# A two-layer graph network on a dense 8192 x 8192 adjacency: no late diagonal product, one ScalarE stop a row, combinations behind the first strip

## The reference

```python
h = maximum(layernorm(x), 0)
T0 = h; T1 = L @ T0; T2 = 2 * (L @ T1) - T0; T3 = 2 * (L @ T2) - T1
x = x + T0 @ w0 + T1 @ w1 + T2 @ w2 + T3 @ w3        # Chebyshev layer, K = 4
h = maximum(layernorm(x), 0)
deg = clip(sum(L, axis=1) + 1, 1)
neigh = (L @ h + h) / deg
out = maximum(concat(h, neigh) @ W + b, 0)
x = x + out / maximum(norm(out, axis=1), 1e-12)      # SAGE layer
```

## Time and profile before

| | |
|---|---|
| median of 3 runs | 2723.29 us |
| lowest, highest | 2719.33, 2724.41 us |
| profiled execution, its own time | 2724.01 us |
| its span | 2722.2 us |
| TensorE matmul busy | 2173.2 us (80%) |
| VectorE busy | 1667.8 us (61%) |
| GpSimd (gather issue) busy | 1269.6 us (47%) |
| ScalarE busy | 688.7 us (25%) |
| moved by DMA | 690.08 MB, mean 253 GB/s |
| mean granted TensorE clock | 0.892 |

### The profile page before, as it was taken

How to read it: one execution, slowest core, us unless ns; L and a number is a source line. 1 busy time by engine, 2 the same in 40 slices (tenths; PEclk the granted TensorE clock), 3 DMA queues, 4 the chain that set the end, 5 groups by cost and what they waited for, 6 DMA issues and landing times.

```text
span 2722.2 us, 29753 instructions
## 1 busy us (share of the span) xinstructions
PE 2173.2 (80%) x12008; PEld 1683.9 (62%) x12008; DVE 1667.8 (61%) x1328; ACT 688.7 (25%) x1667; POOL 1269.6 (47%) x1357
## 2 busy tenths in 40 slices
PE   2567777787888899888886899687867999998785
PEld 1344445566666677767775788566655877775453
DVE  7565555573555555466534575557465687779886
ACT  3342222222221222255111132535121122120000
POOL 4554444434444434074422363534332576667771
PEclk9787777889888899889898899788988999999887
DMA  9797777756766667587744698867766899999995
GB/s 280 263 310 235 248 243 247 247 186 231 269 242 243 200 210 258 171 216 248 263 149 191 234 317 249 241 208 212 257 223 226 266 365 340 332 338 360 364 277 182
DMA packets 220747, 690.08 MB, mean 253 GB/s; under 512 B 47554, under 2 KB 78274, under 8 KB 220610
## 3 DMA queue, kind: packets, MB, share of 16 engines
q0 software_dynamic: 163840, 652.30, 70.2%
q1 hardware_dynamic: 51776, 34.64, 5.0%
q10 hardware_dynamic: 4994, 1.25, 0.3%
HBM read 685.97 MB, written 2.10 MB: 253 GB/s over the span
## 4 chain that ended last, share of the span: by engine, by line
PE 56%; DVE 20%; POOL 7%; issue 6%; DMA 6%; ACT 4%; SPq 1%; ACTq 0%; DVEq 0%; POOLq 0%
PE ps_pair L815 40%; DVE ring L666 17%; PE ps_single L821 10%; POOL ring L408 7%; DMA ring<-in_adj_dram,index 5%; ACT ring L457 3%; PE ps_lin L757 1%; PE ps_lin L760 1%; SPq L379 1%; PE ps_single L719 1%; DMA ring<-in_adj_dram 1%; PE ps_lin L759 0%; PE ps_tr L776 0%; PE ps_lin L773 0%; PE ps_late L730 0%
## 5 line engine op out<-in xcount | busy, mean ns | idle before, releaser
L408 POOL DMA_INDIRECT ring<-in_adj_dram,index x1344 | 1268.1, 944 | 1400.4 <-PE ps_pair L815 514.7
L666 DVE STREAM_TRANSPOSE ring<-ring 128x2048 f32<-128x2048 f32 (+8 forms) x702 | 1466.6, 2134 | 705.6 <-ACT ring L457 605.5
L815 PE MATMUL ps_pair<-ring,vec 128*128 128x256 f32 x5760 | 1356.8, 397 | 266.0 <-DVE ring L666 253.7
L815 PEld LDWEIGHTS ps_pair<-ring,vec 128*128 128x128 f32 x5760 | 1137.4, 200 | 473.2 <-issue 197.8
L821 PE MATMUL ps_single<-ring,vec 128*64 128x256 f32 x4672 | 605.7, 413 | 267.0 <-DVE ring L666 261.3
L457 ACT ACTIVATE ring<-ring 128x1024 f32<-128x1024 f32 (+7 forms) x736 | 576.4, 786 | 405.6 <-DMA ring<-in_adj_dram,index 401.0
L821 PEld LDWEIGHTS ps_single<-ring,vec 128*64 128x64 f32 x4672 | 347.3, 148 | 491.6 <-issue 223.7
L480 ACT ACTIVATE sum_s<-ps_single 128x512 f32<-128x512 f32 x64 | 37.9, 593 | 745.1 <-PE ps_single L821 544.0
L457 ACT ACTIVATION_READ_ACCUMULATOR ring<-ring 128x1 f32 x736 | 139.1, 189 | 0.0
L638 DVE TENSOR_TENSOR res<-res,ps_late 128x256 f32<-128x256 f32 x12 | 5.1, 422 | 178.4 <-PE ps_late L730 178.4
L468 ACT ACTIVATE vec_t<-ps_xt 64x512 f32<-64x512 f32 x32 | 18.7, 584 | 294.5 <-PE ps_xt L709 294.5
(11 more groups left out here) (91 smaller groups left out, 551.3 us busy)
## 6 DMA issues: line engine op xcount, KB each, us to landing
ring<-in_adj_dram,index POOLq DMA_INDIRECT x1344, 7.2
ring<-in_adj_dram SPq DMA_DIRECT2D x160, 96.0 KB
ring<-in_adj_dram SPq DMA_DIRECT2D x160, 64.0 KB
ring<-in_adj_dram SPq DMA_DIRECT2D x160, 32.0 KB, 8.0
out_dram<-vec SPq DMA_DIRECT2D x64, 32.0 KB, 7.9
res<-in_x_dram SPq DMA_DIRECT2D x4, 256.0 KB, 8.2
res<-in_x_dram ACTq DMA_DIRECT2D x4, 256.0 KB, 8.7
tmp<-in_L_gnn_weight_dram ACTq DMA_DIRECT2D x2, 64.0 KB
```

Source lines behind the costliest of these rows:

```text
L408: pool.indirect_dma_start(strip_of(i)[:, g, :], None, adj_q, bass.IndirectOffsetOnAxis(ap=index[:, 0:1], axis=0), element_offset=(QN * (g ...
L666: nc.vector.transpose(blocks, blocks).then_inc(s_turned, 1)
L815: last = nc.tensor.matmul(ps_pair[n % 2][:, cells], vec[:, CB * J + c, :, :], moving, start=(pair == 0), stop=(pair == pairs - 1))
```

## The change

Five things are done:

- **No late product.** `late_product`, both `late_epilogue`s, `copy_diagonal`, `sum_d` and their semaphores are gone (with `ps_late`, whose PSUM becomes `ps_deg`). In sweep 1 only the units of `latest` stand behind. Sweep 2 loads the diagonal block in all 16 rows, as a single with T1: 24 more half-blocks (12.6 MB), and its combination gets the product of `sum_s` (L763 in the old numbering) in 12 more rows, with an evacuation of `ps_single`.
- **ScalarE.** For row n it sums all strips of the row, and the first strip of row n + 1 if its place is free more than two units before the end of row n; then it copies `vec_t`, then it evacuates. In sweep 1 it then stops once a row.
- **TensorE** combines row n not one unit into row n + 1, but up to a whole strip (in sweep 1 after 4 units), as far as the estimated time to the unit that needs the row's result leaves `LATENCY`.
- **VectorE** combines row n after the turning of the strip that follows (`end_step`; in sweep 1 after 8 steps, two strips, of row n + 1) in place of a count of units.
- **Strips** are at most 10 blocks wide in place of 12. In sweeps 2 and 3 there are 88 strips, 76 of them wide, in place of 78 and 66: rows of 11 and 12 blocks are now cut in two.

The diff, cut to its core (the removed functions are named above):

```diff
-WIDE = 12
+WIDE = 10
...
-LATE_BLOCKS = NB - 4
-LATE = 7
-NEXT = 1
-LEAD = 5
+LATENCY = {1: 14.0, 2: 14.0, 3: 20.0, 4: 0.0}
+BLOCK_COST = (0.86, 1.72)
 STORE_LAG = 12
-SUM_LEAD = 4
...
-                (behind if latest in Js or self.has_late and C in Js else early).append((k, Js))
+                (behind if latest in Js else early).append((k, Js))
...
     for C in reversed(range(NB)):
-        first = C + 1 if C < LATE_BLOCKS else C
-        runs = split(first, NB - 1)
+        runs = split(C, NB - 1)
...
-        ahead = {needed_row(rows[n + 1], J) for J in rows[n + 1].units[0][1]}
-        epilogue_at.append(row_start[n + 1] + (n not in ahead))
...
-    begin_at = [min(epilogue_at[n] + LEAD, first_need.get(n, n_units) + 1,
-                    (epilogue_at + [n_units])[n + 1] + NEXT) for n in range(len(rows))]
+    strip_at = list(itertools.accumulate((i for _, i, _ in units), max))
+    cost_to = [0.0] + list(itertools.accumulate(sum(BLOCK_COST[rows[n].kind(J)] for J in Js) for n, _, Js in units))
...
+        need = first_need.get(n, n_units)
+        at = row_start[n + 1]
+        while at < min(units_to[first_strip[n + 1] + 1], row_start[n + 2] - 1) and \
+                cost_to[need] - cost_to[at + 1] >= LATENCY[rows[n].sweep]:
+            at += 1
+        epilogue_at.append(at)
+        ahead = strip_at[at - 1]
+        while ahead < strip_at[at] and free_at[ahead + 1] < at:
+            ahead += 1
+        end_step.append(steps_to[ahead + 1])
...
             for n, row in enumerate(rows):
-                sum_rows(row_start[n] + SUM_LEAD)
+                ahead = first_strip[n + 1]
+                if n + 1 < len(rows) and free_at[ahead] + 2 < row_start[n + 1]:
+                    ahead += 1
+                sum_rows(ahead)
                 if n in x_rows:
...
-                if n - 1 in late_at:
-                    sum_rows(late_at[n - 1] + SUM_LEAD)
-                    act.wait_ge(s_late, late_rows.index(n - 1) + 1)
...
-                    nc.scalar.activation(sum_d[:], ps_single[(n - 1) % 2][:], ACT.Copy).then_inc(s_lateev, 1)
-                sum_rows(row_start[n + 1] + 1)
                 act.wait_ge(s_unit, row_start[n + 1])
...
                 if n in root_rows:
-                    sum_rows(begin_at[n])
+                    sum_rows(steps_to.index(end_step[n]))
...
                     nc.vector.transpose(blocks, blocks).then_inc(s_turned, 1)
-                    u = units_to[i] + (units_to[i + 1] - units_to[i]) * (p + 1) // steps_of[i]
-                    if rows[n].has_late and i + 1 == first_strip[n + 1] and p + 1 == steps_of[i]:
-                        copy_diagonal(n)
-                    if ended < begun and u >= min(begin_at[ended] + 1, n_units):
+                    step = steps_to[i] + p + 1
+                    if ended < begun and step > end_step[ended]:
                         epilogue_end(ended)
                         ended += 1
-                    if begun < len(rows) and ended == begun and u >= begin_at[begun]:
+                    while begun < len(rows) and ended == begun and step >= end_step[begun]:
                         epilogue(begun)
...
-                    if late < len(late_rows) and ended > late_rows[late] and u >= min(late_end_at[late_rows[late]] + LEAD,
-                                                                                      row_start[late_rows[late] + 2]):
-                        late_epilogue(late_rows[late])
...
-                    if n - 1 in late_at and u == late_at[n - 1]:
-                        late_product(n - 1)
-                    if n - 1 in late_at and u == late_end_at[n - 1]:
-                        late_epilogue(n - 1)
...
-                    if row.has_late and row.C in Js:
-                        pe.wait_ge(s_copied, late_rows.index(n) + 1)
```

More of the change, by code:

```diff
@@ L82, in __init__ @@
         self.sweep, self.C, self.pieces, self.final = sweep, C, pieces, final
-        self.has_late = sweep == 1 and C < LATE_BLOCKS
         early, behind = [], []
@@ L207, in needed_row @@
         return row_index[3, J]
-    epilogue_at = []
-    for n in range(len(rows)):
-        if n + 1 == len(rows):
-            epilogue_at.append(n_units)
-            continue
-        ahead = {needed_row(rows[n + 1], J) for J in rows[n + 1].units[0][1]}
-        epilogue_at.append(row_start[n + 1] + (n not in ahead))
     first_need = {}
@@ L223, in cheb_sage_kernel @@
             first_need.setdefault(needed_row(rows[n], J), u)
[L224 to L225 removed]
+    strip_at = list(itertools.accumulate((i for _, i, _ in units), max))
+    cost_to = [0.0] + list(itertools.accumulate(sum(BLOCK_COST[rows[n].kind(J)] for J in Js) for n, _, Js in units))
+    epilogue_at, end_step = [], []
+    for n in range(len(rows)):
+        if n + 1 == len(rows):
+            epilogue_at.append(n_units)
+            end_step.append(steps_to[-1])
+            continue
+        need = first_need.get(n, n_units)
[8 more added lines that the diff above has]
+        end_step.append(steps_to[ahead + 1])
     def sums_of(n):
@@ L441, in _, with sum_rows @@
             summed = [0]
-            def sum_rows(u):
-                while summed[0] < len(sum_strips) and strip_first[sum_strips[summed[0]]] < u:
+            def sum_rows(strip):
+                while summed[0] < len(sum_strips) and sum_strips[summed[0]] < strip:
                     i = sum_strips[summed[0]]
@@ L711, in transpose_vector @@
                 xts[0] += 1
-            def late_product(n):
-                C = rows[n].C
-                need_rows(n + 1)
-                for c in range(CB):
-                    half = F * (c % 2)
-                    last = nc.tensor.matmul(ps_single[n % 2][half:half + F, :], vec[:, CB * C + c, 1, :],
-                                            diagonal(C, c), start=(c < 2), stop=(c >= CB - 2))
-                last.then_inc(s_late, 1)
-            def late_epilogue(n):
-                late = late_rows.index(n)
-                pe.wait_ge(s_lateev, late + 1)
-                if late:
-                    pe.wait_ge(s_lateadd, late)
-                for c in range(CB):
-                    D = sum_d[:, P * c:P * c + P]
-                    last = nc.tensor.matmul(ps_late[:, c, :, :], D, rhs_s2[:], start=True, stop=True)
-                last.then_inc(s_latelin, 1)
             def epilogue(n):
```

49 lines of the change are left out of this document (3 added, 46 removed).

## The result

| | before | after |
|---|---|---|
| median of 4 runs each, us | 2721.47 (2719.33 to 2724.41) | **2499.06** (2497.35 to 2504.45) |
| profiled execution / its span, us | 2724.0 / 2722.2 | 2497.35 / 2495.5 |
| mean granted clock | 0.892 | 0.931 |

The ratio is 0.9185 [0.9168, 0.9203]. The forecast was 2522 (2440 to 2625), so the sum is off by 23 us. The terms behind the sum were further off: sweep 1 gained 87 us more than forecast, and sweeps 2 and 3 lost 63 more.

What follows compares the result with a forecast made beforehand. Sweep 1 was taken to be bound by two program-order stops, not an engine. Sweep 1 -209, sweep 2 +4, sweep 3 -6, last +10 sum to -201 us: 2523 from the profiled 2724.0, 2522 as median; range 2440 to 2625.

Steps and rivals of the forecast that it cites:

- two stops in order of program: Sweep 1: waits at VectorE's late addition and ScalarE's copy of vec_t bind it, not an engine; removing them saves 209 us.
- ScalarE's stop: Sweep 1, row C = 6: ScalarE stands 21.87 us at vec_t's copy, second strip's sums behind; TensorE then waits 9.61.
- The first stop: Sweep 1, row C = 6: VectorE stands 12.96 us before the late addition, next row's turning behind; TensorE stands 6.99.
- First the prices: Unit costs for the sum: pair half-block 1.88 us, single 1.04, a unit 3.8 or 2.1, turning a half-block 1.1.
- T+17.2, T+35, T+49.7: Sweep 1, rows C = 1 to 7, us from row start: VectorE's combination done, two strips turned, TensorE's five further units done.
- more than forecast: Rival, chance 0.15: loads flow, rows 1 to 7 at 48.5 us, 8 to 12 at 56; 286 us less, 2438.
- 25 + 19 - 10 = +34: Sweep 2, diagonal: 24 singles +25 us, the sum_s product in 12 more rows +19, idle time filled by added products -10.
- -48 + 18 = -30: Sweep 2, narrower strips: stops of rows C = 5 and 4 go, -48 us; new waits at C = 6 and 7, +18.
- VectorE's combination ahead of the next strip's turning costs back about 8: Sweep 3: this cost of about 8 us against about 14 saved by cutting rows C = 10 and 11, giving -6.
- Half the gain: Rival, chance 0.18: VectorE's new wait and low clock keep sweep 1's rows 1 to 7 at 61 us; 2621 in all.
- The gathers: Rival, chance 0.06: GpSimd's queue binds sweeps 2 and 3; 80 more gathers cost 99 us, giving 2621.
- Slower: Rival, chance 0.03: ScalarE's sums ahead of the evacuation hold up TensorE's combination in 16 rows, 395 us more, 2917.

Runs made afterwards that it cites:

- old_places_w12: The kernel before without the late product, with ScalarE's new order; combinations in their old places, strips up to 12 blocks; quick chip: 2483.82 us, ratio 0.9133.
- late_off_act: The kernel before without the late product, with ScalarE's new order, old combination places, strips up to 12 blocks; slow chip: 2905.98 us, ratio 0.9593.
- old_places_w10: The kernel before without the late product, with ScalarE's new order, old combination places, strips up to 10 blocks; quick chip: 2408.10 us, ratio 0.8853.
- old_places_w8: The kernel before without the late product, with ScalarE's new order, old combination places, strips up to 8 blocks; quick chip: 2349.96 us, ratio 0.8646.
- second set: Quick-chip runs of the changed kernel again (2497.47 us) and, with old combination places, strips up to 12, 10 and 8 blocks (2483.82, 2408.10, 2349.96 us).
- tensor_place_new: Against late_off_act_w10, TensorE's combination alone moved to the changed kernel's place, VectorE's and ScalarE's left as before; slow chip: 3103.28 us, ratio 1.0274.
- late_off_act_w10: The kernel before without the late product, with ScalarE's new order, old combination places, strips up to 10 blocks; slow chip: 2860.33 us, ratio 0.9436.
- late_off: The kernel before with only the late product removed, its diagonal moved to sweep 2; slow chips: 3000.48 us, ratio 0.9877; repeated, 2977.94 us, 0.9865.

## Why the prediction was right, and where it was not

**Right as a total, by two errors that offset.** The forecast of 2522 is 23 us above 2499, inside the range, and the cause it named for the gain, two stops in order of program in sweep 1, is borne out as a pair: old_places_w12 takes only the late product and ScalarE's old order away, and its sweep 1 takes 805 us, not 1110. ScalarE's stop is also shown alone, by late_off_act. The first stop's own part stays open: with the late product go the late stop, the ring places of the held block (some 40 us) and 33 us of TensorE's work (19.4 + 13.3 in the earlier trace rows), and no run takes these apart.

**Sweep 1: -209 forecast, -296 measured.** The mechanism was right, and the prices were not. The term that was mis-sized goes back to "First the prices": I took pair, single and combination from means over the whole kernel or from a stretch at the low clock, and the change itself lifts the clock. In rows 8 to 12, before and after (groups by line in the windows 583.2 to 945.8 and 425.1 to 681.3):

```profile
L815 PE MATMUL ps_pair<-ring,vec 128*128 128x256 f32 x801 | 202.1, 413 | 70.7 <-DVE ring L666 70.7
```

```profile
L736 PE MATMUL ps_pair<-ring,vec 128*128 128x256 f32 x801 | 177.2, 380 | 3.4 <-DVE ring L621 3.4
L742 PE MATMUL ps_single<-ring,vec 128*64 128x256 f32 x484 | 55.5, 382 | 0.1
```

A pair half-block is 177.2/100 = 1.77 us there, not 1.88, a single one 55.5/60.5 = 0.92, not 1.04, and the combination 4.7, not 7.7. My own sum for C = 10 with these, 20 x 1.77 + 12 x 0.92 + 4.7 + 1.0, gives 52.1 us; 50.3 was measured, and I had 58.8. For rows 1 to 7 the chain T+17.2, T+35, T+49.7 holds step by step in row C = 5: VectorE begins to turn at T+14.1 (3.1 us earlier, the combination), has both strips at T+31.8, and the row ends 14.9 us later, at T+46.7 (323.8). The 1.7 us of low clock wasn't there. The average of 48.5 is then set by the loads, near the bound of 47.3. By group: row 0 16 forecast, 19 measured (58 to 39); rows 1 to 7 114 and 139; rows 8 to 12 68 and 106; rows 13 to 15 11 and 32, the last since TensorE's busy time fell too, 189.3 to 176.3, with the clock from 0.92 to 1.00. This is what the rival "more than forecast" said of sweep 1 (48.5 for rows 1 to 7), with too little for the others.

**Sweep 2: +4 forecast, +26 measured.** old_places_w12 and w10 split it. The diagonal, forecast as 25 + 19 - 10 = +34 us, came to +61 (556 to 617, with the old places and 12 blocks; ScalarE's order is in it too). The narrower strips, -48 + 18 = -30, came to -55. The places of the combinations, to which I gave no cost in this sweep, are +16. In the +61 TensorE's busy time grew by 40 us (475.5 to 515.2), near the 25 + 19 of the forecast; what failed is "Some of the remaining idle time is filled by the added products: -10", for its idle time grew by 21 instead (80.5 to 101.9). The two stops of C = 5 and 4 are gone as forecast (46.8 and 42.6 us for 62.7 and 65.9 of the earlier trace rows), and the stop moved to C = 7 and 6 as forecast, but larger than 18:

```profile
1052.12 14.71 PE L736 MATMUL ps_pair<-ring,vec 128*128 128x256 f32 x56 [8.38 <-DVE ring L621]
1070.05 0.94 POOL L392 DMA_INDIRECT ring<-in_adj_dram,index  x1 [30.66 <-PE ps_pair L736]
1092.25 3.33 PE L736 MATMUL ps_pair<-ring,vec 128*128 128x256 f32 x7 [19.54 <-DVE ring L621]
```

GpSimd's gather is held 30.66 us until a strip is free, and TensorE stands 8.38 and 19.54 us, 27.9 in all, and 9.4 more in C = 6. old_places_w8, where TensorE doesn't stand at all in these rows, shows that this was the choice of 10 and not a price of narrow strips.

**Sweep 3: -6 forecast, +35 measured.** This is the one term with the wrong sign. The strips gave -21 (I had -14), and the late product and ScalarE's order together +9 (728 to 737), for which I have no account. The step that failed is "VectorE's combination ahead of the next strip's turning costs back about 8": the places cost 47. I counted the place of VectorE's four operations but not that it would stand there for TensorE's, which the change had moved too, nor ScalarE's root with sums queued behind it. How the 47 split between the three engines' places isn't shown on the quick chip.

**Last sweep: +10 forecast, +9 measured.** VectorE waits 39.5 us in 16 waits for L700 (above), 2.5 each, which is the 16 x 2.5 of the forecast; it waited 13.8 in 5 before. Only part of it reached the path; the places alone cost 13 in the second set.

**The other rivals.** Half the gain didn't come: TensorE's waits in rows 1 to 7 of sweep 1 were 2.2 us on average (36.8 in 17), and the clock stayed up, 0.94 there. The gathers did not bind (second set); "no run here shows 320 KB" overlooked that the kernel before has strips of 5 blocks too, in row C = 10 of sweep 2 and row C = 4 of sweep 3. "Slower" (sums ahead of an evacuation) didn't appear in sweep 1; ScalarE's waits for landings did grow, from 401.0 to 532.7 us in the whole kernel, but TensorE's combination stood for an evacuation only once in sweep 1, 1.2 us. A mechanism of the slower side did exist, but it was another: TensorE's late combination in tensor_place_new, which alone outweigh the rest of the gain on a slow chip.

## What to carry to other kernels

When a change removes stops, price what is left at the clock of a stretch without stops, not at the kernel's mean. When a producer is moved later because it can afford it, look at the consumer: on an engine that runs in order everything behind the consumer waits with it, so move both or neither, and try each alone, since a good part of a change can hide a part that costs (here 89 us, where the rest of the change gained 312). When a ring limits a stretch, size the pieces so that a whole neighbour fits beside them: 8 blocks in place of 12, with the combinations left where they were, is 5.9% faster than the changed kernel (2349.96 against 2497.47).

## What I had not expected of the hardware

The same programs took longer on two of the three chips of these sets, and not all by the same share: the kernel before 11 and 12%, late_off_act 17% (2905.98 against 2483.82 as old_places_w12), late_off_act_w10 19% (2860.33 against 2408.10 as old_places_w10). The durations of instructions that don't hang on TensorE's clock are the same (a sum of ScalarE 786 ns in the kernel before on the first chip and in late_off on a slow one, a gather's issue 944 and 942); what differs is the idle time between them. TensorE's waits that the profile puts down to nothing it shows ("issue"), in the kernel before on the first chip:

```profile
PE ps_pair L815 <- issue: 5.6, 1, 5.6
PE ps_single L821 <- issue: 4.7, 3, 1.7
```

and in late_off on a slow one:

```profile
PE ps_single L820 <- issue: 191.9, 171, 9.9
PE ps_pair L814 <- issue: 157.1, 86, 25.4
```

One and the same kernel shows it as well: as old_places_w12 on the quick chip 14.5 us in 4 such waits, as late_off_act on the slow one 338 in 249, leaving out the wait ahead of the first product. 208 of these waits are of at most 1.7 us; some stand inside a run of independent products, such as two of 1.68 and 1.02 us just before 329.5 and 330.9 us.

The mean granted clock of that kernel is 0.880 there, against 0.932 on the quick chip. What makes the gaps isn't settled: no experiment was made on it. The order of the kernels was the same on both kinds of chip where they can be compared (late_off_act 0.9593 and 0.9133, late_off_act_w10 0.9436 and 0.8853), but a slow chip shows less than half of the gain. That the gaps take most from the kernels that otherwise wait least is a guess.
